# Attention and feed-forward block on one core: an earlier load of one x unit, the diagonal block copied by ScalarE, another order of the weight sums

## What is computed

```
K = x @ Wk + bk            # 16 heads of 16 channels; Q = x
V = x @ Wv + bv            # 16 heads of 64 channels
attn = softmax(Q K^T + causal mask)
o = attn @ V
x = layernorm(x + x + gelu(o) @ Wf + bf)
g, u = x @ Wg^T, x @ Wu^T  # int weights times 1/127
x = layernorm(x + (silu(g) * u) @ Wd^T)
```

## Time and profile before

| | us |
|---|---|
| median of 3 runs (lowest, highest) | 1849.84 (1847.09, 1851.43) |
| the profiled execution's own time | 1849.75 |
| its span in the profile | 1848.0 |
| PE busy / PEld | 1762.1 / 961.4 |
| DVE / ACT / POOL busy | 1396.5 / 1050.4 / 1221.8 |
| mean granted clock of TensorE | 0.991 |

### The profile page before, as it was taken

The page is one execution under the profiler, slowest core; times in us unless marked ns, Lnnn a source line. Parts: engine busy times, 40 slices in busy tenths (PEclk is TensorE's granted clock), DMA queues, the critical chain, the costliest instruction groups (busy, mean ns, idle before and its releaser), DMA issues. The chain is left out here.

```text
span 1848.0 us, 37611 instructions
## 1 busy us (share of the span) xinstructions
PE 1762.1 (95%) x10304; PEld 961.4 (52%) x10304; DVE 1396.5 (76%) x3417; ACT 1050.4 (57%) x1375; POOL 1221.8 (66%) x1146
## 2 busy tenths in 40 slices
PE   7999999999999999999999999888889999999996
PEld 5444444444444444444444444333466767676763
DVE  4787877778787787777778787886467878787864
ACT  2465665665565565665666565555545555555552
POOL 3488888888888888888888888999512222222221
PEclk9999999999999999999999999999999999999998
DMA  9675657556565655646556565563477565756500
GB/s 323 160 232 160 181 141 203 161 161 188 142 176 170 168 160 159 195 139 185 169 148 196 145 174 143 144 183 99 138 201 175 172 170 172 169 172 170 171 24 23
DMA packets 261152, 303.16 MB, mean 164 GB/s; under 512 B 28240, under 2 KB 177872, under 8 KB 261072
## 3 DMA queue, kind: packets, MB, share of 16 engines
q1 hardware_dynamic: 261072, 302.19, 58.3%
HBM read 174.20 MB, written 127.93 MB: 163 GB/s over the span
## 5 line engine op out<-in xcount | busy, mean ns | idle before, releaser
L802 POOL TENSOR_TENSOR weight_sum<-weight_sum,weights 128x512 f32<-128x512 f32 (+1 forms) x444 | 731.9, 1649 | 151.9 <-DVE weight_sum L1347 115.3
L1161 ACT ACTIVATE weights<-ring 128x1024 f32<-128x1024 f32 x576 | 570.7, 1026 | 221.2 <-PE ring L846 217.8
L846 PE MATMUL o_acc<-weights,v_pair 128*64 128x512 f32 (+3 forms) x3072 | 586.3, 501 | 17.1 <-POOL weights L757 16.4
L837 POOL TENSOR_TENSOR h_lo<-hidden,h_hi 128x512 f16<-128x512 f32 x96 | 114.4, 1193 | 390.2 <-ACT h_hi L1099 390.2
L1312 DVE TENSOR_REDUCE part_max<-ring 128x2 f32<-128x1024 f32 x256 | 301.0, 1217 | 86.4 <-PE ring L846 86.4
L846 PEld LDWEIGHTS o_acc<-weights,v_pair 128*64 128x64 f32 x3072 | 188.3, 136 | 302.7 <-issue 257.0
L1321 DVE CUSTOM_DVE_ANT_0 scrap<-ring,causal,part_max 128x256 bf16<-128x256 f32 (+3 forms) x512 | 251.3, 547 | 70.7 <-PE ring L846 70.4
L1321 DVE CUSTOM_DVE_ANT_0 scrap<-ring,causal 128x128 bf16<-128x128 f32 (+3 forms) x512 | 225.1, 486 | 91.1 <-PE ring L846 90.6
L846 PE MATMUL ring<-q_stack,k_stack 50*128 50x512 f32 (+3 forms) x1536 | 264.3, 382 | 26.1 <-DVE part_max L1312 17.6
L846 PE MATMUL ring<-k_stack,q_stack 48*128 48x512 f32 (+3 forms) x1536 | 256.9, 373 | 0.1
L846 PE MATMUL ring<-wf_sb,g 128*128 128x256 f32 x1024 | 230.5, 380 | 2.6 <-DVE y_pre L1416 1.7
(11 more groups left out here) (125 smaller groups left out, 2070.1 us busy)
## 6 DMA issues: line engine op xcount, KB each, us to landing
v_pairs<-v_unit SPq DMA_DIRECT2D x64, 512.0 KB, 3.5
v_pair<-v_pairs SPq DMA_DIRECT2D x64, 512.0 KB, 5.1
o_heads<-o_pair SPq DMA_DIRECT2D x64, 512.0 KB, 3.2
g<-o_heads SPq DMA_DIRECT2D x16, 2048.0 KB, 8.1
den_wide<-reciprocals SPq DMA_DIRECT2D x32, 1024.0 KB, 13.3
q_stack<-q_rows SPq DMA_DIRECT2D x128, 192.0 KB, 3.7
k_stack<-k_rows SPq DMA_DIRECT2D x128, 192.0 KB, 4.4
q_rows<-x_hi SPq DMA_DIRECT2D x28, 512.0 KB, 3.6
```

The lines of the kernel that those rows point to most:

```text
L802: pool.tensor_tensor(dst, other, weights(t), ALU.add).then_inc(s_add, 1)
L837: pool.tensor_tensor(h_lo[:, f], h32[f % 2][:], h_hi[:, f], ALU.subtract).then_inc(s_hl, 1)
L846: return nc.tensor.matmul(o, l, r, start=start, stop=stop)
L1161: nc.scalar.activation(W[i][:], bank_of("t", i)[:], ACT.Exp).then_inc(s_w, 1)
```

## The change

The third unit's x is loaded right after the first load of stacks, ahead of the early v and k stores, and ScalarE rounds it in burst 0 of step 0 instead of burst 3. `mask(0)` loses its first select; ScalarE copies the masked diagonal block of W[0] into `acc0` in burst 3 (`copy_diagonal`), and the denominators wait for that copy. Group 10 is added after group 2 and ahead of group 3 and of `x_low`; it waits only for `begin_sum`, `carry_sum` waits for it, and group 7 waits for `carry_sum`. In the last two steps VectorE makes the sums of groups 1 and 2, and GpSimd that of group 3.

```diff
-        ADDS = (1, 2, 3, 10, 7, 8, 9, 11)
+        ADDS = (1, 2, 10, 3, 7, 8, 9, 11)
@@ sync, ahead of the loop
             load_stacks(0, 0)
+            load_x(ALONE, True)
             store_early_v(0, 0)
             store_early_k(0, 1)
             store_early_v(0, 1)
             store_early_k(1, 1)
             store_early_v(0, 2)
-            load_x(ALONE, True)
             store_early_v(0, 3)
@@ gpsimd, mask
-                if i == 0:
-                    if rt >= 2:
-
-                        pool.wait_ge(s_den, n - 1)
-                        settle(pool, s_passed["pool"])
-                    pool.affine_select(out=acc0[rt % 2][:, :, 0:P], in_=W[0][:, :, 0:P], compare_op=ALU.is_ge, fill=0.0,
-                                       base=0, pattern=[[0, 2], [1, P]], channel_multiplier=-1)
@@ gpsimd, add
-                if t == 10:
-
-                    pool.wait_ge(s_add1, 2 * (n + 1))
-                    if rt >= PAIRS - 2:
-
-                        pool.wait_ge(s_add, NA * n + added(3))
-                elif t != 1:
+                if t == 1 and rt >= 2:
+
+                    pool.wait_ge(s_den, n - 1)
+                if t in (10, 7):
+
+                    pool.wait_ge(s_add1, 2 * n + (1 if t == 10 else 2))
+                if t != 1:
 
                     pool.wait_ge(s_add, NA * n + added(t) - 1)
@@ gpsimd, attend
                     mask(2, *m)
                     if r < PAIRS:
-                        for t in (1, 2, 3):
-                            add(t, *m)
+                        add(1, *m)
+                        add(2, *m)
+                    add(10, *m)
+                    add(3, *m)
                 if r % 4 == 0 and unit_beside(r, it) is not None:
                     x_low(unit_beside(r, it))
                 if now:
-                    add(10, *m)
                     add(7, *m)
@@ tensor, denominators
+                pe.wait_ge(s_add0, n + 1)
@@ scalar
+            def copy_diagonal(rt, n):
+
+                act.wait_ge(s_sel, NM * n + masked(0))
+                if rt >= 2:
+
+                    act.wait_ge(s_den, n - 1)
+                copy(acc0[rt % 2][:, :, 0:P], W[0][:, :, 0:P]).then_inc(s_add0, 1)
@@ scalar, attend
+                    if b == 3 and LEAD <= r < PAIRS + LEAD:
+                        copy_diagonal(r - LEAD, n - LEAD)
                     for what, i in uses(b):
                         if what == "t" and LEAD <= r < PAIRS + LEAD:
                             exponent(i, r - LEAD, n - LEAD)
-                    if b == 3 and r % 4 == 0 and unit_beside(r, it) is not None:
+                    if b == (3 if r else 0) and r % 4 == 0 and unit_beside(r, it) is not None:
                         x_high(unit_beside(r, it), r == 0)
@@ vector
             def carry_sum(rt, n):
                 dve.wait_ge(s_w, NU * n + use_of(6) + 1)
                 dve.wait_ge(s_add1, 2 * n + 1)
+                dve.wait_ge(s_add, NA * n + added(10))
@@ vector, first_half_sum
-                for t in (1, 2, 3):
+                for t in (1, 2):
                     w = width_of(t)
                     dst = acc0[rt % 2][:, :, BANK - w:BANK]
                     dve.wait_ge(s_sel, NM * n + masked(t))
+                    dve.wait_ge(s_den, n - 1)
```

More of the change, by code:

```diff
@@ L290, in build @@
         s_pv = sem("weights_used")
+        s_add0 = sem("diagonal_block_copied")
         s_add1 = sem("sums_begun")
```

## The result

The changed kernel takes 1864.58 us, the median of 5 runs (1860.79 to 1866.05), against 1850.5 us before (5 runs, 1847.09 to 1852.5): a ratio of 1.0074, 95% interval 1.0059 to 1.009. That is 14.1 us slower, where 1850.0 was forecast and 1861 was the upper end. The profiled execution took 1864.27 us, with a span of 1862.5 us and a mean granted clock of 0.991 as before.

A forecast was written before the change was run, and what follows sets the result against it. TensorE paces nearly all of the span, so GpSimd's idle time counts only where TensorE waits for it. 1849.75 - 5.6 + 7.8 + 3.6 - 5.5 = 1850.05, given as 1850.0 us; eight-in-ten range 1839 to 1861.

The forecast's parts named there:

- early load: First step: earlier x of the third unit removes TensorE's 4.34 us wait and lifts the clock; gain 5.6 us.
- copy on ScalarE: Diagonal block copy ahead of the sixth exponent fits in ScalarE's idle 0.35 us; cost nothing, bounds 0 to 0.1 us a step.
- longer first sums: Steps with jobs: group 2's add is in flight at every `begin_sum`, 0.6 us in four steps, +7.8 us.
- x_low and second sum: r % 4 = 0 steps: x_low goes first at equal starts, `carry_sum` ends later, scores lose 0.28 us more; +3.6 us.
- steps without jobs, end: Steps 57 to 63 and the end: GpSimd, 0.36 us less loaded per step, delays TensorE less; -5.5 us.
- rival B: x_low steps: VectorE's `carry_sum` starts first, x_low is blocked, TensorE's job waits 1.07 us; 1860.3 us, chance 0.23.
- GpSimd's idle time: Sign to look for: GpSimd's waiting before its adds falls far below 115 us.
- C: Steps with jobs: the sums do not meet, so 7.8 + 3.6 us are not paid; 1838.6 us, chance 0.20.
- D: First step: x lands no earlier, or stores behind it delay step 1's stacks; 1855.6 us, chance 0.08.
- E: First sums wait for the whole add, 0.28 us more in each of 13 turns; 1853.7 us, chance 0.05.

The follow-up runs named there:

- x_low-first kernel: The changed kernel with GpSimd's x_low moved ahead of its add of group 3; 1850.17 us (ratio 0.9996).
- all parts: Kernel before plus early load, ScalarE's copy, group 2 held for the first sum in steps with jobs, x_low ahead of group 3; 1831.93 us.
- tie-turned kernel: The changed kernel with VectorE's second sum waiting for group 3 instead of group 10, so x_low starts first; 1857.03 us.

## Why the prediction was wrong

By its own sum, from 1849.75 us:

| step | forecast | measured | from |
|---|---|---|---|
| early load | -5.6 | -5.2 | first sum of step 2; the load alone gave -5.7 |
| copy on ScalarE | 0 | 0 | sixth exponent 0.82 instead of 0.81 us behind the first sum |
| longer first sums | +7.8 | +7.4 | turn of x_low-first kernel less that of before, 0.57 x 13 |
| x_low and second sum | +3.6 | +14.6 | turn of after less that of x_low-first, 1.12 x 13 |
| steps without jobs, end | -5.5 | -2.6 | -3.6 and +1.0 |

The terms add up to +14.2 of the 14.5 us between the two profiled executions; the 0.3 is left in the loop. "0.57 x 13" and "1.12 x 13" take the mean of eight turns; read over the thirteen turns themselves, the two are +8.0 and +14.3.

*The load* was right in place and size: x_hi at 29.61 us (near 30 was forecast), x_lo ready at 33.2, no wait for it, the clock at its upper level.

*The first sums* were right (the term +7.8): 1.45 to 1.63 us in all four kinds of step of the loop, with group 2 at 1.28 us. From a first sum with r % 4 = 2 to the next with r % 4 = 0 it is 40.28 us (634.92 to 675.20), 39.89 before and 40.2 forecast. That TensorE pays for each tenth on a first sum, which the prediction took from two rows whose idle times differ by 0.18 us for sums that differ by 0.34, holds over whole turns: first sums of a turn longer by 0.64, 1.71 and -0.61 us (x_low first, copy alone, all parts) go with turns longer by 0.57, 1.66 and -0.70.

*The step that failed is the one on x_low (the term +3.6).* The arithmetic was right: both starts were put at one moment, 2.19 us behind the first sum, and they came 2.19 and 2.20 us behind it. What was wrong was to settle the tie by the earlier trace rows, where GpSimd went first. That row is of another pair of operations, in it GpSimd's start is recorded 0.01 us ahead, and it does not carry over: x_low, recorded 0.01 to 0.06 us behind, lost all 13 times, and another 13 times in the kernel with the order alone. TensorE then waited 13 times for x_lo, 13.5 us, where the forecast had no wait, and the term measured +14.6 instead of +3.6. With the order reversed the forecast's mechanism held again, as the tie-turned kernel shows (0.73 us a turn less; the forecast had 0.79 between the two cases), and the rest is 0.39 us a turn where the forecast had 0.28. So the cause was seen, priced and named as rival B, at 1860.3 us and with 0.23, and taken for the less likely. The profiled execution is 4.0 us above B, about 0.4 from the load, 0.6 from the loop, 2.9 from the steps without jobs. The range ended at the middle of B, which left no room for an error of the terms that B shares with the forecast; it should have gone through to B's far side.

*The steps without jobs* were mis-sized. I counted 0.36 us a step for the select, and did not ask whom GpSimd, once earlier, would meet there. It meets the first sum with the add of group 1 in three of the seven steps 57 to 63. Copy alone and order alone give next to nothing in these steps (148.1 and 148.6 us against 148.8), together 3.6 us. A step there was to take 17.8 us; from 57 to 62 it takes 16.6 to 19.8, now with a meeting and now without, and 17.9 in the mean (18.2 before). So most of the forecast for the single step did come; of the 3.6 us, 1.7 are in these six steps and the rest in 63 and 64. What is missing is in what was counted once or by feel, and no run separates that. The +1.0 us of the end is no effect that is shown: that stretch lies between 533.5 and 537.5 us in the twelve profiles.

*GpSimd's idle time* before its adds was to be far below 115 us; it is 75.7 + 55.0 us. The order took away one long wait and made two, since group 7 waits for the second sum as group 10 did.

*The other rivals:* C (sums that don't meet) and D (a load that brings nothing) are refuted by the rows above. E read the 0.15 us as a tail of the add that is free only at times. The rows say otherwise: in every meeting in these traces the first sum ends 1.08 or 1.09 us after the add, whether it has been waiting for 0.3 or for 1.7 us. That is the whole of its own 1.23 us but for 0.15, so the block is full, and it was already so in the kernel before. The price of 0.28 us a turn for E therefore doesn't exist. This is what the Trainium skill states (SBUF — State Buffer, section "SBUF: two separate sides": the one that starts first has the shared port pair for its whole instruction), and the traces here agree, but for the 0.15 us.

## What to carry to other kernels

Where two engines block each other, look not at busy shares but at the distance of their starts, and treat a distance below the length of the edit as a cliff: 0.36 us less work on the idle engine cost 22 us here. When two starts are computed to fall together, the outcome is not known from another pair of instructions; write the order into the kernel with a wait, or move one of them by the length of a small job. And before an engine is relieved, hold what it would start sooner: the load and the copy, whose effects alone add up to +16.8 us (-5.7 and +22.5), came to -18.4 us (1831.93 against 1850.36) with one wait of GpSimd on the first sum and x_low moved ahead, and the wait without the move gave only -3.4. The order of group 10 is not part of that kernel.

## What the runs showed of the hardware

A blocked instruction costs its whole length behind the other, less 0.15 us, on either engine: the first sum (1.23 us alone) ends 1.08 us after the add, x_low (2.37) 2.21 us after the second sum (680.05 to 682.26). VectorE's reductions of the scores are not part of it: the pair at 636.42 us in the kernel after takes 2.34 us with GpSimd's add of group 10 running beside it (636.72 to 638.00), and 2.35 us in the earlier trace rows.

Below 0.02 us the starts in a trace don't tell who is first. x_low lost with starts 0.01 to 0.08 us behind the second sum, and won 0.07 us ahead of it. But the add of group 1 wins against the first sum although its row stands 0.02 us behind, as in the kernel with all parts:

```profile
1187.34 2.93 DVE L1355 TENSOR_TENSOR weight_sum<-weights 128x1024 f32<-128x1024 f32 x1
1187.36 1.83 POOL L802 TENSOR_TENSOR weight_sum<-weights 128x768 f32<-128x768 f32 x1
```

and loses 0.03 us behind, as in the kernel after:

```profile
1196.93 1.23 DVE L1348 TENSOR_TENSOR weight_sum<-weights 128x1024 f32<-128x1024 f32 x1
1196.96 2.88 POOL L796 TENSOR_TENSOR weight_sum<-weights 128x768 f32<-128x768 f32 x1
```

What sets this offset between kinds of instruction is open; each pair was consistent with itself in all twelve traces.
